# A decoder layer in two-pass attention: a reordered opening whose first queries go through DRAM, the second pass masked by a GpSimd select, and the values of both key tiles in one visit

## What is computed

```python
x = x + self_attn(_layernorm(x))          # rope on q, k; causal mask; softmax; @ Wo.T
x = x + cross_attn(_layernorm(x), ctx)    # no mask; softmax; @ W_proj + b_proj
x = x + moe(_layernorm(x))                # top 2 of 8 experts per sequence, gelu, combine
# inside either attention:
attn = jnp.einsum('bhqd,bhkd->bhqk', q, k) * scale
attn = jnp.where(causal, -jnp.inf, attn)  # self-attention alone
out = jnp.einsum('bhqk,bhkd->bhqd', jax.nn.softmax(attn, axis=-1), v)
```

## Time and profile before

| | |
|---|---|
| median of 3 runs | 212.4 us (211.24 to 214.91) |
| the profiled execution | 211.94 us |
| its span, first to last instruction | 210.2 us |
| mean granted clock of TensorE | 0.967 |
| busy: PE, DVE, ACT, POOL | 181.0, 139.0, 104.4, 51.7 us |

### The profile page before, as it was taken

The page is one execution under the profiler, slowest core; times in us unless marked ns, Lnnn a source line. Parts: engine busy times, 40 slices in busy tenths (PEclk is TensorE's granted clock), DMA queues, the critical chain, the costliest instruction groups (busy, mean ns, idle before and its releaser), DMA issues.

```text
span 210.2 us, 4262 instructions
## 1 busy us (share of the span) xinstructions
PE 181.0 (86%) x1552; PEld 115.6 (55%) x1552; DVE 139.0 (66%) x337; ACT 104.4 (50%) x222; POOL 51.7 (25%) x101
## 2 busy tenths in 40 slices
PE   0749389838999999999999899899999999799994
PEld 0413367625555656654655554364565455398994
DVE  3799478832456678779889888979887527524220
ACT  2130023313456465556466576666866575695441
POOL 4460028895000042011011003001106107107040
PEclk9999979995699999999999999999999999999999
DMA  5815431474504301340340340210070070070630
GB/s 147 226 49 151 140 102 50 138 177 120 134 2 127 102 2 56 101 115 9 100 122 5 92 134 5 72 44 2 5 227 5 2 225 5 4 221 25 173 107 25
DMA packets 25292, 18.64 MB, mean 89 GB/s; under 512 B 2424, under 2 KB 23416, under 8 KB 24696
## 3 DMA queue, kind: packets, MB, share of 16 engines
q1 hardware_dynamic: 24048, 17.79, 30.5%
q10 hardware_dynamic: 1224, 0.59, 1.0%
HBM read 11.36 MB, written 2.10 MB: 64 GB/s over the span
## 4 chain that ended last, share of the span: by engine, by line
PE 64%; DVE 19%; DMA 7%; issue 2%; ACTq 2%; POOL 2%; ACT 2%; SPq 1%; POOLq 0%; DVEq 0%
PE psV L872 12%; PE psA L824 11%; PE psB L851 10%; PE psV L934 6%; DVE negmax L592 5%; DMA stackQ<-maxT 4%; PE psA L917 4%; PE psM L882 3%; PE psB L856 3%; PE psA L829 3%; PE psM L754 3%; DVE stats L528 2%; PE psM L892 2%; ACTq L680 2%; DMA stackQ<-hid 2%
## 5 line engine op out<-in xcount | busy, mean ns | idle before, releaser
L708 ACT ACTIVATE E<-psB 128x512 f32<-128x512 f32 x112 | 62.6, 597 | 53.9 <-PE psB L856 32.0
L592 DVE TENSOR_REDUCE negmax<-psA 128x2 f32<-128x512 f32 (+1 forms) x112 | 72.6, 682 | 21.0 <-PE psA L829 19.0
L824 PE MATMUL psA<-stackK,stackQ 72*128 72x256 bf16 (+1 forms) x256 | 44.8, 268 | 8.5 <-DVE negmax L592 4.5
L851 PE MATMUL psB<-stackQ,stackK 74*128 74x256 bf16 (+1 forms) x256 | 42.3, 266 | 4.6 <-DMA stackQ<-maxT 4.5
L872 PE MATMUL psV<-E,V 128*9 128x256 f32 (+1 forms) x512 | 36.6, 358 | 0.0
L824 PEld LDWEIGHTS psA<-stackK,stackQ 72*128 72x128 bf16 x256 | 21.2, 101 | 25.2 <-DVE negmax L592 12.8
L851 PEld LDWEIGHTS psB<-stackQ,stackK 74*128 74x128 bf16 x256 | 23.9, 100 | 11.2 <-DMA stackQ<-maxT 5.2
L447 POOL TENSOR_SCALAR rstd<-mv 128x2 f32<-128x2 f32 x12 | 2.8, 235 | 107.7 <-DVE mv L532 107.6
L934 PE MATMUL psV<-w2s,hid 128*128 128x128 f32 x128 | 16.4, 277 | 0.8 <-ACT hid L735 0.8
L934 PEld LDWEIGHTS psV<-w2s,hid 128*128 128x128 f32 x128 | 15.7, 192 | 1.5 <-issue 1.2
L829 PE MATMUL psA<-mask,ident 128*128 128x256 bf16 (+1 forms) x48 | 15.9, 332 | 0.0
(11 more groups left out here) (111 smaller groups left out, 218.8 us busy)
## 6 DMA issues: line engine op xcount, KB each, us to landing
stackK<-scratch SPq DMA_DIRECT2D x18, 192.0 KB
...
```

The costliest lines, as they stand in the source:

```text
L592: dve.tensor_reduce(negmax[:, b, h:h + nh, t], psA[:, bank].rearrange("p (h k) -> p h k", h=nh), AX_X, ALU.max, negate=True).then_inc(a_ta ...
L708: act.activation(dst, psB[:, bank].rearrange("p (h q) -> p h q", h=dst.shape[1]), ACT.Exp, scale=SCALE).then_inc(b_taken, 1)
L824: last = pe.matmul(psA[:, bank, i * keys:(i + 1) * keys], stackQ[0:ROWS, b, h, t * P:(t + 1) * P], stackK[0:ROWS, b, h, 0:keys], start=(s ...
L851: last = pe.matmul(psB[:, bank, i * n:(i + 1) * n], stackK[:, b, h, t * P:(t + 1) * P], stackQ[:, b, h, q0:S], start=(s == 1 or i == 0), s ...
```

## The change

1. **Opening.** `keep_warm` has 10 matmuls instead of 16 and stands twice, around the context turns and products of batch 0, which come forward; it waits for the constants alone. The constants are made earlier on POOL. The q parts of batch 0 no longer go by nine DMAs of ACT: ACT writes parts 0 and 1, then part 2, to `scratch`, and reads them back spread over `stackQ` in two DMAs. Batch 1 does the same with one write and one read.
2. **First pass.** `max_rows` of job 0 stands at half 7 instead of 8, and the DRAM writes and reads of batch 2 stand behind it at halves 9 and 10 (before: 7 and 8); batch 3 follows at 15 and 17 (before: 12 and 13). `qk_self` of batches 2 and 3 uses `psB`; DVE's rotation is a step of its own (`rope`), and POOL's splitting is cut into single instructions placed half by half (`rope_split`, `k_split`).
3. **Mask of the second pass.** `mask16T` and its matmuls go. After the exponential of a unit that holds a diagonal block, POOL sets the entries above the diagonal of `E` to 0 with an affine select of 128 x (4 x 128) fp32, twice per group of self-attention (32 in all); `values` waits for `e_masked` instead of `b_taken`.
4. **Values.** Both key tiles are multiplied in one visit, at the later of the two halves.

```diff
-WARM = 16
+WARM = 10
...
-    start = [("ln_stats", 0, 0), ("ln_apply", 0, 0), ("ln_turn", 0, 0), ("ln_stats", 0, 1), ("ln_apply", 0, 1),
-             ("ln_stats", 0, 2), ("ln_stats", 0, 3), ("constants", 0, 0), ("qk_self", 0, 0), ("ln_turn", 0, 1),
-             ("qk_cast", 0, 0), ("qk_self", 0, 1), ("ln_apply", 0, 2), ("ln_apply", 0, 3), ("stack_fill", 0, 0),
-             ("stack_fill", 0, 1), ("keep_warm", 0, 0)]
+    start = [("ln_stats", 0, 0), ("constants", 0, 0), ("ln_apply", 0, 0), ("ln_turn", 0, 0), ("ln_stats", 0, 1),
+             ("ln_apply", 0, 1), ("ln_stats", 0, 2), ("ln_stats", 0, 3), ("qk_self", 0, 0),
+             ("ln_turn", 0, 1), ("qk_cast", 0, 0), ("qk_self", 0, 1), ("stack_put", 0, 0), ("ctx_turn", 1, 0),
+             ("ctx_turn", 1, 1), ("keep_warm", 0, 0), ("stack_fill", 0, 0), ("stack_get", 0, 0), ("k_cross", 1, 0),
+             ("v_cross", 1, 0), ("keep_warm", 0, 1), ("stack_put", 0, 1), ("stack_fill", 0, 1), ("stack_get", 0, 1),
+             ("ln_apply", 0, 2)]
     put(0, "ln_turn", 0, 2)
-    put(1, "ln_turn", 0, 3)
-    put(1, "qk_self", 0, 2)
-    put(2, "ctx_turn", 1, 0)
-    put(2, "v_self", 0, 0)
-    put(3, "k_cross", 1, 0)
-    put(3, "ctx_turn", 1, 1)
+    put(1, "ln_apply", 0, 3)
+    put(1, "v_self", 0, 0)
+    put(2, "qk_self", 0, 2)
+    put(3, "rope", 0, 2)
+    put(3, "ln_turn", 0, 3)
     put(4, "k_cross", 1, 1)
-    put(4, "v_cross", 1, 0)
     put(5, "qk_self", 0, 3)
-    put(5, "v_cross", 1, 1)
-    put(6, "ctx_turn", 1, 2)
-    put(7, "k_cross", 1, 2)
-    put(7, "ctx_turn", 1, 3)
-    put(8, "k_cross", 1, 3)
-    put(9, "v_cross", 1, 2)
-    put(10, "v_cross", 1, 3)
-    for b, half in ((2, 7), (3, 12)):
-        put(half, "stack_write", 0, b)
-        put(half + 1, "stack_read", 0, b)
+    put(6, "v_cross", 1, 1)
+    put(7, "ctx_turn", 1, 2)
+    put(7, "max_rows", 0, 0)
+    put(8, "rope", 0, 3)
+    put(9, "k_cross", 1, 2)
+    put(9, "ctx_turn", 1, 3)
+    put(10, "v_cross", 1, 2)
+    put(12, "k_cross", 1, 3)
+    put(13, "v_cross", 1, 3)
+    put(9, "stack_write", 0, 2)
+    put(10, "stack_read", 0, 2)
+    put(15, "stack_write", 0, 3)
+    for n in range(10):
+        put(3, "rope_split", 0, 2, n)
+        put((8, 8, 9, 9, 10, 10, 11, 12, 13, 14)[n], "rope_split", 0, 3, n)
...
-        put(16 + 3 * b, "k_split", 1, b)
-        put(17 + 3 * b, "stack_write_k", 1, b)
+        for n in range(4):
+            put(16 + 4 * b + n, "k_split", 1, b, n)
+        put(19 + 4 * b, "stack_write_k", 1, b)
...
-        put(n + 2 * NG, "max_rows", s, b)
+        if j > 0:
+            put(n + 2 * NG, "max_rows", s, b)
+        if j == 1:
+            put(n + 2 * NG + 1, "stack_read", 0, 3)
...
-        if 0 <= n < NJOB * NG:
-            order.append(("values", *divmod(n // NG, NB), n % NG, h))
+        if h == 1 and 0 <= n < NJOB * NG:
+            order.append(("values", *divmod(n // NG, NB), n % NG))
...
+        def thrice(s, b, i, n):
+
+            src = scratch[s, b, 0, i:i + n]
+            return bass.AP(src.tensor, src.offset, [[NH * S, n * HD], [0, NPART], [1, NH * S]])
...
-                if kind == "stack_fill" and (s == 1 or b > 0):
+                if kind == "stack_fill" and s == 1:
                     for i in range(NPART):
                         for r in range(NPART):
-                            fill_q(b, i, r, parts_q[b] if s == 1 else parts_q_self[b])
+                            fill_q(b, i, r, parts_q[b])
+                if kind == "stack_get" and b == 1:
+                    sp.wait_ge(scr_q_self[b], 16)
+                    read_q(s, b)
...
+            pool.memset(ident16[:, :], 0.0)
+            then(pool.memset(mask16[:, :, :], 0.0))
...
+                if kind == "rope_split":
+
+                    w, n = (1, g) if g < 5 else (0, g - 5)
+                    cs, sn = rot[:, b % 2, 0, w], rot[:, b % 2, 1, w]
+                    if g == 0:
+                        pool.wait_ge(rope_first, b + 1)
+                    if n == 0:
                         then(pool.tensor_tensor(cs, cs, sn, ALU.add))
-                        split(cs, parts[:, b, w], ready)
+                    else:
+                        split(cs, parts[:, b, w], (parts_q_self[b], parts_k_self[b])[w], n - 1)
...
+                if kind == "scores_exp" and s == 0 and st["u"] >= 1:
+
+                    pool.wait_ge(b_taken, unit + 1)
+                    t = st["u"] - 1
+                    diagonal = E[:, (job * NG + g) % 3, :, t, t * P:(t + 1) * P]
+                    pool.affine_select(out=diagonal, in_=diagonal, compare_op=ALU.is_ge, fill=0.0, base=0,
+                                       pattern=[[0, GH], [1, P]], channel_multiplier=-1).then_inc(e_masked, 1)
...
+                if kind == "rope" or (kind == "qk_self" and b < 2):
+                    if b == 0:
+                        dve.wait_ge(rope_in, 16)
+                    dve.wait_ge(qk_full, b + 1)
+                    if b >= 2:
+                        dve.wait_ge(parts_q_self[b - 2], NPART)
+                    rope_terms(psB[:, b % 2], rot[:, b % 2], rope_first)
...
-                if kind == "stack_fill" and s == 0 and b == 0:
-                    for i in range(NPART):
-                        for r in range(NPART):
-                            act.wait_ge(parts_q_self[b], i + 1)
-                            act.dma_start(stackQ[i * BLOCK + r:(i + 1) * BLOCK:NPART, b],
-                                          parts[:, b, 0, i]).then_inc(q_in[b], 16)
+                if kind == "stack_put" and b == 0:
+                    act.wait_ge(parts_q_self[b], 2)
+                    act.dma_start(scratch[0, b, 0, 0:2].rearrange("i p t -> p i t"),
+                                  parts[:, b, 0, 0:2]).then_inc(scr_q_self[b], 16)
+                    act.wait_ge(parts_q_self[b], NPART)
+                    act.dma_start(scratch[0, b, 0, 2], parts[:, b, 0, 2]).then_inc(scr_q_rest, 16)
+                if kind == "stack_put" and b == 1:
+                    act.wait_ge(parts_q_self[b], NPART)
+                    act.dma_start(scratch[0, b, 0].rearrange("i p t -> p i t"),
+                                  parts[:, b, 0]).then_inc(scr_q_self[b], 16)
+                if kind == "stack_get" and b == 0:
+                    act.wait_ge(scr_q_self[b], 16)
+                    act.dma_start(stackQ[0:2 * BLOCK, b], thrice(0, b, 0, 2)).then_inc(q_in[b], 16)
+                    act.wait_ge(scr_q_rest, 16)
+                    act.dma_start(stackQ[2 * BLOCK:ROWS, b], thrice(0, b, 2, 1)).then_inc(q_in[b], 16)
...
-                    pe.wait_ge(consts, 5)
-                    pe.wait_ge(parts_q_self[b], NPART)
+                    pe.wait_ge(consts, 4)
...
+                    if unit < 2:
+                        pe.wait_ge(rope_first, unit + 3)
...
-                                         stackQ[:, b, h, q0:S], start=(s == 1 or i == 0), stop=(s == 1),
-                                         skip_group_check=True)
-                    if s == 0:
-                        blocks = psB[:, bank].rearrange("p (h q) -> p h q", h=len(heads))[:, :, 0:P]
-                        last = pe.matmul(blocks, ident16[:, :], mask16T[:, 0:len(heads), :], start=False, stop=True,
-                                         skip_group_check=True)
+                                         stackQ[:, b, h, q0:S], start=True, stop=True)
                     last.then_inc(b_full, 1)
                 if kind == "values":
-                    grp, t = job * NG + g, st["u"]
-                    if t == 0:
-                        if grp >= 2:
-                            pe.wait_ge(v_taken, grp - 1)
-                        if g == 0:
-                            taken("v_self" if s == 0 else "v_cross", s, b)
-                        if grp == 0:
-                            pe.wait_ge(v_init, 1)
-                            pe.wait_ge(v_zeroed, 1)
+                    grp = job * NG + g
+                    if grp >= 2:
+                        pe.wait_ge(v_taken, grp - 1)
+                    if g == 0:
+                        taken("v_self" if s == 0 else "v_cross", s, b)
+                    if grp == 0:
+                        pe.wait_ge(v_init, 1)
+                        pe.wait_ge(v_zeroed, 1)
+                    if s == 0:
+                        pe.wait_ge(e_masked, 2 * (grp + 1))
+                    else:
                         pe.wait_ge(b_taken, b_units_until(grp))
-                    q0 = P if s == 0 and t == 1 else 0
-                    for i in range(GH):
-                        last = pe.matmul(psV[i * VW:i * VW + VC, grp % 2, q0:S], V[:, s, b, t, g * GH + i, :],
-                                         E[:, grp % 3, i, t, q0:S], start=(t == 0), stop=(t == 1),
-                                         skip_group_check=True, tile_position=(0, i * VW))
-                    if t == 1:
-                        last.then_inc(v_full, 1)
+                    for t in range(NT):
```

(6 more changed lines are left out.)

96 lines of the change are left out of this document (41 added, 55 removed).

## The result

The changed kernel takes 210.84 us (median of 20 runs, 204.56 to 216.72) against 211.54 us (20 runs, 209.89 to 214.91) for the kernel before. The comparison by the fastest runs gives a ratio of 0.973, 95% interval 0.967 to 0.979; for the changed kernel it rests on the two runs that lie within 1.5% of its fastest (204.56 and 207.21), so the median says better what an execution usually takes. The forecast was 199.7, range 194.0 to 205.5: the sign was right, the time lies outside the range. The runs spread over 12 us, those of before over 5, and follow TensorE's mean granted clock: 0.956 in the run of 204.56, 0.897 in that of 216.72. The profiled execution takes 209.88 (span 208.2, mean clock 0.918), 2.1 less than the one of before, and 10.2 more than forecast.

A forecast was written before the change was run, and what follows sets the result against it. It took late fills, the maxima wait and low clock to bound the early part, then PE and DVE with little slack. Gains 6.4 + 5.3 + 1.7 + 0.4 + 0.6, less 1.0 and 1.2, took 211.94 to 199.7 us; range 194 to 205.5.

The forecast's parts named there:

- Wait for the maxima, 4.2: Before the second pass: maxima leave ahead of batch 2's reads, so PE no longer waits for them; 4.2 us gained.
- the low clock of job 0, 4.15: Second pass of job 0: without the idle, 8.3 us at half speed become 4.15.
- First pass, nothing of its own: First pass of job 0: DVE sets its length; small gains and losses cancel, within 1.0 us either way.
- Opening, 2.2: Start of the kernel: q through DRAM brings first scores at 21.8 instead of 24.0; 2.2 us gained.
- 2.0 to 3 for landing no later than that: Opening: batch 0's k fills, issued by 18.6, land within 2.0 to 3 us, no later than q at 21.8.
- costs nothing on the path: Early second pass: batch 2's moved DRAM writes and reads, needed before half 16, add no time.
- Masks and visits in jobs 0 and 1, 5.3 and 1.7: Second pass: job 0 gains 5.3 us, including 4.15 from the clock; job 1 gains 1.7 from masks and visits.
- Costs, 2.2: Second pass: later jobs' maxima arriving late cost 1.0 us, POOL's selects, including rstd queued behind them, 1.2.
- The next four jobs, 0.4 gained: Four jobs after job 1: 1.2 us counted from saved masks, less 0.8 for the merged visit; 0.4 gained.
- whether DVE would starve: Cross-attention in the next four jobs: the merged visit makes DVE run dry longer and PE then wait; 0.8 us net.
- rival (d): Late maxima or low clock stays, from PE's pauses in a DVE-bound first pass; 208.0 us, chance 0.05.
- From 152.5 on, 0.6 gained: End of the kernel, no first pass running: merged visits in five groups at 0.12 to 0.17; 0.6 us gained.

The follow-up runs named there:

- the longer warm-up: Second keep_warm has 32 matmuls instead of 10, against a kernel with selects only in jobs 0-1, merged visits in 0, 1, 6, 7, earlier batch-2 k write: 200.18 us.
- mask-sized filler: Opening, selects and two values visits, plus an unread mask-sized matmul in each first-half second-pass visit, against the same kernel without those matmuls: 206.13 us against 208.67.

## Why the prediction was wrong

- **Wait for the maxima, 4.2, and the low clock of job 0, 4.15**: right. PE does not wait, and job 0 runs at 1.00. There is some luck in the second: five of the versions above had a low stretch of about 3.4 us in job 0 after a wait for the q read of batch 2, in the changed kernel the clock held through 2.05.
- **First pass, nothing of its own, since DVE sets it**: the pass took 20.3 where the sum had 19.9, but at a mean clock of 0.82. With the clock at 1.00 it takes 17.9 (the longer warm-up), so DVE alone does not set it, and its low clock cost over 2 us that no term of the sum held.
- **Opening, 2.2**: the step "2.0 to 3 for landing no later than that" for k failed. The fill issued before 17.89 landed 5.70 later, beside the other fills, q's reads and q's write: 23.73, 1.9 late. It cost in total 2.3 at the start of the second pass. The row of q's fill, 4.15, was the nearest one and was used only as the outer bound.
- **Traffic of batch 2 "costs nothing on the path"**: wrong. Its q read was issued at 44.61 and landed 7.52 later: 2.05 of wait in job 0, then 0.94 for batch 3's in job 1. I had counted halves to the last issue, not to the landing. Issuing earlier gave 1.5 back.
- **Masks and visits in jobs 0 and 1, 5.3 and 1.7**: job 0 took 17.1 (44.03 to 61.09) where the sum had 16.1, job 1 16.4 where it had 15.2. The DMA waits, 2.05 in job 0 and 0.94 and 0.87 in job 1, are more than the difference in both.
- **Costs, 2.2**: of the right kind. The maxima of job 2 came 0.87 late, and the share of POOL is 0.1 to 0.5 a job at full clock; a select was 0.635, not 0.75. The forecast way is there: the chain passes a select on its way to `rstd` (82.38 to 83.92). A second way was missed: DVE's own `xn` goes from 0.35 to 0.59 us beside a select.
- **The next four jobs, 0.4 gained**: this is the step that failed, by 8.9 us: they took 74.6 (77.50 to 152.10) instead of 65.7. With the opening alone, at full clock, the same four take 66.1 (79.70 to 145.82), so nearly all of the 8.9 goes with the low clock and the pauses before it. I asked whether DVE would starve, and priced that at 0.8; at full clock the merged visit costs nothing in job 2. What I did not ask is what TensorE's clock does when it is given less work, or the same work in fewer and later pieces, in jobs that DVE bounds. I had it as rival (d), but placed it in the first pass, gave it 0.05, and argued that the low stretch of before followed an idle of over 4 us. The Trainium skill (TensorE: Matmul & The Clock Gate, A second HAM failure mode) had said that short pauses between groups of matmuls, as banks are cycled, can do it; the pauses of 0.98 and twice 1.48 ahead of the three low stretches, and the mask-sized filler that took the low stretches away, agree with it. No run here shows how long or how dense the pauses must be: in job 1 pauses of 0.94 and 0.87 did not bring a fall, nor did 2.05 in job 0.
- **From 152.5 on, 0.6 gained**: 1.6 (208.2 - 152.1 against 210.2 - 152.5). Jobs 6 and 7 took 15.1 and 13.2 with the merged visit, 16.3 and 13.3 without.
